# A state-space stage on one core: row statistics moved ahead, the first chunk reordered, sixteen gathers spread over four chunks

## What is computed

```python
x = x + _L0_ffn_ref(_layernorm(x), ...)      # two experts' rows per token are gathered and added
x = x + _L1_attn_ref(_layernorm(x), ...)     # the state space; it adds its own input, the normed x
# _L1_attn_ref(x):
xn = x * rsqrt(mean(x * x) + EPS) * norm_w
xi, res = split(xn @ in_proj_w)
xi = silu(conv1d(xi) + conv_b)               # 4 taps
delta, Bm, Cm = split(xi @ x_proj_w)
delta = softplus(delta @ dt_proj_w + dt_proj_b)
state = exp(delta * -exp(A_log)) * state + delta * Bm * xi    # a scan over 256 steps, 16 states
y = (sum over the states of state * Cm) + xi * D
out = (y * silu(res)) @ out_proj_w + x
```

## Time and profile before

| | us |
|---|---|
| median of 3 runs | 1331.45 |
| lowest, highest | 1325.25, 1331.91 |
| the profiled execution, its own time | 1329.53 |
| its span in the trace | 1327.7 |
| DVE busy in the span | 938.6 (71%) |
| PE busy | 1060.4 (80%) |
| POOL busy | 836.1 (63%) |
| ACT busy | 748.2 (56%) |

### The profile page before, as it was taken

One profiled execution on the slowest core, in us unless ns is written; L12 is line 12 of the kernel. 1 busy time (PEld: TensorE's weight loads), 2 busy tenths in 40 slices (PEclk: granted clock), 3 DMA queues, 4 the chain that ended last, 5 costly groups with the idle time before them and its releaser, 6 DMA issues. The chain is left out here.

```text
span 1327.7 us, 20305 instructions
## 1 busy us (share of the span) xinstructions
PE 1060.4 (80%) x4202; PEld 616.8 (46%) x4203; DVE 938.6 (71%) x2289; ACT 748.2 (56%) x1827; POOL 836.1 (63%) x602
## 2 busy tenths in 40 slices
PE   5888966489999865888988889897774239999995
PEld 4666744367777622323333333333222225555563
DVE  6999998533333325899999999999997525555573
ACT  4768755265555447867677675866422115555542
POOL 2333268657157278968788888879670677347276
PEclk9998878599999977899999999898897559999997
DMA  9994012336335224343445444354440136435345
GB/s 266 156 152 128 1 15 23 36 55 91 64 74 87 61 41 105 128 138 120 159 127 160 126 144 152 119 172 125 150 142 0 41 58 97 78 77 95 77 69 104
DMA packets 140459, 133.22 MB, mean 100 GB/s; under 512 B 14578, under 2 KB 121698, under 8 KB 140258
## 3 DMA queue, kind: packets, MB, share of 16 engines
q1 hardware_dynamic: 107106, 115.55, 33.0%
q0 software_dynamic: 33280, 16.86, 11.4%
HBM read 98.66 MB, written 31.60 MB: 98 GB/s over the span
## 5 line engine op out<-in xcount | busy, mean ns | idle before, releaser
L1766 POOL TENSOR_TENSOR ss_HC<-ss_Hs,ss_Cb 128x512 f32<-128x512 f32 x256 | 317.9, 1272 | 89.9 <-PE ss_Y L1540 68.5
L1540 PE MATMUL ss_Y<-ss_HC,g_ident 128*128 128x512 f32 x512 | 268.0, 641 | 45.7 <-POOL ss_HC L1766 37.9
L1835 DVE TENSOR_TENSOR_SCAN ss_Hs<-ss_dA,ss_dBu 128x512 f32<-128x512 f32 x256 | 297.0, 1201 | 5.4 <-ACT ss_dA L1682 4.9
L852 POOL DMA_INDIRECT rows<-m_XS,g_slot x128 | 181.8, 1420 | 67.1 <-issue 36.2
L1151 PE MATMUL m_x_UP<-g_m_w,m_x_gT 128*128 (+1 forms) x532 | 204.8, 491 | 6.7 <-issue 3.2
L1682 ACT ACTIVATE ss_dA<-ss_delta,g_A 128x510 f32<-128x510 f32 x256 | 167.7, 712 | 57.8 <-DVE ss_Hs L1835 57.6
L1540 PEld LDWEIGHTS ss_Y<-ss_HC,g_ident 128*128 128x128 f32 x512 | 89.5, 196 | 208.8 <-POOL ss_HC L1766 151.4
L1827 DVE TENSOR_TENSOR ss_dBu<-ss_duP,ss_Bb 128x512 f32<-128x512 f32 x256 | 163.1, 683 | 19.2 <-DMA ss_Bb<-bc_rows 14.9
L1171 PEld LDWEIGHTS m_x_DP<-g_m_w,m_x_hT 128*128 128x128 f32 (+1 forms) x908 | 131.5, 189 | 81.2 <-issue 40.1
L1171 PE MATMUL m_x_DP<-g_m_w,m_x_hT 128*128 (+3 forms) x908 | 161.8, 296 | 5.4 <-issue 2.5
L1131 POOL DMA_INDIRECT g_X<-out_rows,g_slot x64 | 99.6, 1557 | 79.9 <-DMA out_rows<-m_x_YO 57.4
(11 more groups left out here) (265 smaller groups left out, 1825.7 us busy)
## 6 DMA issues: line engine op xcount, KB each, us to landing
ss_Bb<-bc_rows SPq DMA_DIRECT2D x64, 512.0 KB, 4.9
ss_Cb<-bc_rows SPq DMA_DIRECT2D x64, 512.0 KB, 3.8
rows<-g_Z SPq DMA_DIRECT2D x2, 5031.0 KB, 55.4
m_x_G<-rows SPq DMA_DIRECT2D x156, 64.5 KB
out_rows<-m_x_YO SPq DMA_DIRECT2D x156, 64.0 KB
g_m_w<-in_w_up SPq DMA_DIRECT2D x1, 2816.0 KB, 10.8
g_m_b<-in_b SPq DMA_DIRECT2D x1, 2160.0 KB, 11.8
g_X<-in_x SPq DMA_DIRECT2D x4, 512.0 KB, 6.5
```

Source lines behind the costliest of these rows:

```text
L852: self.nc.gpsimd.indirect_dma_start(self.XG, bass.IndirectOffsetOnAxis(self.rt.slot[k][:, t:t + 1], 0), self.XS[:, t, :], None, compute_op ...
L1540: ins = nc.tensor.matmul(Yp[:, h, :], ident[:], HC[n % 2][:, h, :], start=False, stop=n == N - 1)
L1766: nc.gpsimd.tensor_tensor(HC[n % 2][:, h, :], Hs[n % 4][:, h, :], Cb[g % 2][:, n % 2, :], ALU.mult).then_inc(hc_ready.sem, 1)
L1835: v_.tensor_tensor_scan(Hs[n % 4][:, h, :], dA[n % NA][:, h, :, :].rearrange("p s t -> p (s t)"), dBu[:, h, :], 0.0, ALU.mult, ALU.add).th ...
```

## The change

Three things are changed.

- A class `StateRows` takes over the row scales, in three batches: tiles 0 to 15, 16 to 23 and 24 to 31. Batch 0 is done in the last steps of the experts: four groups of four `bn_stats` after the steps NX-1 to NX+2, the moments after NX+3, an ACT Sqrt after NX+4, and the reciprocal with its Newton step after NX+5. Batch 1 goes into chunk 0 (DVE after n = 6 and n = 10, ACT after n = 8), batch 2 into chunk 4 (DVE after n = 1 and n = 3, ACT after n = 2). The empty block that waited for the weights is gone; the engines wait themselves.
- The first chunk is reordered. Its gate product moves behind its softplus, chunk 1's rows are normalised early and written to a second xT, the exponential of A moves behind the first silu, and the softplus runs by halves of 512 columns: ACT does Abs, Exp, Identity for one half and then the other, DVE takes the relu, the sums and du by halves. `copy_du` sits between the two halves of dA.
- Of POOL's 32 gathers at the start, 16 stay (tiles 16 to 23). The 16 for tiles 24 to 31 are issued one each after n = 8, 10, 12 and 14 of chunks 0 to 3. `chunks` becomes a plain loop, with no hardware loop.

```diff
+                def closing(s):
+                    if s == NX + 4:
+                        ahead.scalar_root(act, 0)
...
+                def closing(s):
+                    lo, hi = ahead.batches[0]
+                    q = (hi - lo) // 4
+                    if s == NX - 1:
+                        dve.wait_ge(early, 16 * n_early * 2)
+                    if NX - 1 <= s < NX + 3:
+                        ahead.vector_stats(dve, 0, lo + q * (s - NX + 1), lo + q * (s - NX + 2))
+                    if s == NX + 3:
+                        ahead.vector_moments(dve, 0)
+                    if s == NX + 5:
+                        ahead.vector_scales(dve, 0)
...
+    def vector_moments(self, dve, b):
+        v, link = self.nc.vector, Chain(dve, self.chain)
+        lo, hi = self.batches[b]
+        k = hi - lo
+        dve.wait_ge(self.measured.sem, self.measured.after(b))
+        for t in range(k):
+            ins = v.bn_aggr(self.mv[:, t, :], self.st[:, t, :])
+        link(ins)
+        v.tensor_scalar(self.ve[:, 1, 0:k], self.mv[:, 0:k, 1], 1.0 + EPS, EPS * EPS, ALU.mult, ALU.add)
+        v.tensor_scalar(self.ve[:, 0, 0:k], self.mv[:, 0:k, 1], EPS, None, ALU.add).then_inc(self.shifted.sem, 1)
+        v.tensor_copy(self.mean[:, lo:hi], self.mv[:, 0:k, 0])
+
+    def scalar_root(self, act, b):
+        lo, hi = self.batches[b]
+        act.wait_ge(self.shifted.sem, self.shifted.after(b))
+        self.nc.scalar.activation(self.t2[:, :, 0:hi - lo], self.ve[:, :, 0:hi - lo], ACT.Sqrt).then_inc(self.rooted.sem, 1)
+
+    def vector_scales(self, dve, b):
+        v, link = self.nc.vector, Chain(dve, self.chain)
+        lo, hi = self.batches[b]
+        k = hi - lo
+        y, t2 = self.scales[:, :, lo:hi], self.t2[:, :, 0:k]
+        dve.wait_ge(self.rooted.sem, self.rooted.after(b))
+        link(v.reciprocal(y, t2))
+        link(v.tensor_tensor(t2, y, y, ALU.mult))
+        link(v.tensor_tensor(t2, t2, self.ve[:, :, 0:k], ALU.mult))
+        link(v.tensor_scalar(t2, t2, -0.5, 1.5, ALU.mult, ALU.add))
+        link(v.tensor_tensor(y, y, t2, ALU.mult))
+        v.scalar_tensor_tensor(self.shift[:, :, lo:hi], self.mean[:, lo:hi].unsqueeze(1).to_broadcast([P, 2, k]),
+                               -1.0, y, ALU.mult, ALU.mult)
+        v.tensor_scalar(self.lift[:, lo:hi], self.scales[:, 0, lo:hi], 1.0, None, ALU.add).then_inc(self.scaled.sem, 1)
...
+                pe.wait_ge(loaded.sem, loaded.after(n_loaded - 1))
                 turn(0, Q[1])
-                project(0, q)
-                project_gate(0, [dBu[:, h, :] for h in range(2)])
+                project(0, 0, q)
                 pe.wait_ge(weights_ready, 1)
                 pe.wait_ge(padded, 1)
                 for h in range(2):
                     convolve(0, h, q[h])
-                project_dbl(0, 0)
-                project_dt(0)
+                first_dbl(Q[0][0:DT, :], w_lr, (0, 1))
+                first_dbl(Q[1][0:2 * N, :], w_bc, (0,))
+                pe.wait_ge(lr_copied.sem, lr_copied.after(0))
+                nc.tensor.matmul(Q[0][:], w_dt[:, 0:P], lr[:], start=True, stop=True).then_inc(dt_ready.sem, 1)
+                first_dbl(Q[1][0:2 * N, :], w_bc, (1,))
                 turn(1, Z[0])
-                project(1, Z)
+                pe.wait_ge(bc_copied.sem, bc_copied.after(0))
+                nc.tensor.matmul(Q[1][:], w_dt[:, P:2 * P], lr[:], start=True, stop=True).then_inc(dt_ready.sem, 1)
+                pe.wait_ge(xT_copied.sem, xT_copied.after(1))
+                project_gate(0, 0, Z)
+                pe.wait_ge(z_copied.sem, z_copied.after(0))
+                project(1, 1, q)
                 for h in range(2):
-                    convolve(1, h, Z[h])
+                    convolve(1, h, q[h])
...
+                def first_log():
+                    for h in range(2):
+                        act.wait_ge(dt_ready.sem, dt_ready.after(0, h + 1))
+                        nc.scalar.activation(ez[:, h, :], Q[h][:], ACT.Abs, bias=dt_b[:, h:h + 1]).then_inc(first_logs, 1)
+                        act.wait_ge(first_logs, 3 * h + 1)
+                        nc.scalar.activation(ez[:, h, :], ez[:, h, :], ACT.Exp, scale=-1.0).then_inc(first_logs, 1)
+                        act.wait_ge(first_logs, 3 * h + 2)
+                        nc.scalar.activation(tz[:, h, :], ez[:, h, :], ACT.Identity, bias=unit[:, 0:1]).then_inc(first_logs, 1)
+                    for h in range(2):
+                        nc.scalar.activation(ln[:, h, :], ez[:, h, :], ACT.Ln, bias=1.0).then_inc(first_logs, 1)
...
+                        if n == 0 and h == 0 and not at(c, 0, 1):
+                            copy_du(c)
...
+                        if n == 0 and not at(c, 0, 1):
+                            silu_xi(1, 1, q)
+                            silu_gate(0, 0)
...
+                        if (c, n) == (0, 8):
+                            rows_of.scalar_root(act, 1)
+                        if (c, n) == (4, 2):
+                            rows_of.scalar_root(act, 2)
...
+                act.wait_ge(loaded.sem, loaded.after(n_loaded - 1))
                 normalise(0, 0)
-                copy_xT(0, Q[1][:])
+                copy_xT(0, 0, Q[1][:])
+                normalise(1, 0)
                 act.wait_ge(padded, 1)
                 copy_in(0, q)
-                copy_gate(0, 0, [dBu[:, h, :] for h in range(2)])
+                add_normalised(0)
+                add_normalised(1)
                 silu_xi(0, 0, q)
+                nc.scalar.activation(A[:], A[:], ACT.Exp).then_inc(powered, 1)
                 copy_dbl(0)
-                add_normalised(0)
-                copy_dt(0, 0)
                 act.wait_ge(units_set, 2)
-                log_dt(0)
-                normalise(1, 0)
-                add_normalised(1)
-                copy_xT(1, Z[0])
+                first_log()
                 act.wait_ge(negated, 1)
                 act.wait_ge(cleared, NA)
                 powers(0, 0, 0)
-                copy_du(0)
-                for n in range(1, NA - 1):
-                    powers(n, 0, 0)
-                copy_in(1, Z)
-                silu_xi(1, 1, Z)
-                silu_gate(0, 0)
+                copy_in(1, q)
+                powers(1, 0, 0)
+                copy_gate(0, 0, Z)
+                powers(2, 0, 0)
                 chunks(act, scan)
...
-                for k in range(2):
-                    for t in range(n_early, T):
-                        nc.gpsimd.indirect_dma_start(X[:, t * D:(t + 1) * D], None, Y,
-                                                     bass.IndirectOffsetOnAxis(rt.slot[k][:, t:t + 1], 0),
-                                                     compute_op=ALU.add).then_inc(gathered, 16)
-                    pool.wait_ge(gathered, 16 * (T - n_early) * (k + 1))
+                def gather(k, t, done):
+                    nc.gpsimd.indirect_dma_start(X[:, t * D:(t + 1) * D], None, Y,
+                                                 bass.IndirectOffsetOnAxis(rt.slot[k][:, t:t + 1], 0),
+                                                 compute_op=ALU.add).then_inc(done, 16)
+
+                for t in range(*soon):
+                    gather(0, t, gathered)
+                pool.wait_ge(gathered, 16 * n_soon)
+                for t in range(*soon):
+                    gather(1, t, gathered)
 
...
+                        i = 4 * c + (n - 8) // 2
+                        if n >= 8 and n % 2 == 0 and i < 2 * n_late:
+                            if i == n_late:
+                                pool.wait_ge(late_gathered, 16 * n_late)
+                            gather(i // n_late, late[0] + i % n_late, late_gathered)
...
+                        if (c, n) == (0, 6):
+                            dve.wait_ge(gathered, 16 * 2 * n_soon)
+                            rows_of.vector_stats(dve, 1, *soon)
+                            rows_of.vector_moments(dve, 1)
+                        if (c, n) == (0, 10):
+                            rows_of.vector_scales(dve, 1)
+                        if (c, n) == (4, 1):
+                            dve.wait_ge(late_gathered, 16 * 2 * n_late)
+                            rows_of.vector_stats(dve, 2, *late)
+                            rows_of.vector_moments(dve, 2)
+                        if (c, n) == (4, 3):
+                            rows_of.vector_scales(dve, 2)
...
+                def first_relu(h):
+                    dve.wait_ge(first_logs, 3 * h + 1)
+                    v_.tensor_scalar(delta[0][:, h, :], Q[h][:], dt_b[:, h:h + 1], 0.0, ALU.add, ALU.max).then_inc(z_copied.sem, 2)
+
+                def first_rest(h):
+                    dve.wait_ge(first_logs, 3 * h + 3)
+                    v_.scalar_tensor_tensor(tz[:, h, :], tz[:, h, :], -1.0, ez[:, h, :], ALU.add, ALU.subtract).then_inc(first_sums, 1)
+
+                first_relu(0)
+                dve.wait_ge(turned.sem, turned.after(1))
```

(15 more changed lines are left out.)

150 lines of the change are left out of this document (57 added, 93 removed).

## The result

The changed kernel took 1316.38 us (median of 10 runs, 1313.25 to 1320.61), the kernel before 1331.37 us beside it: ratio 0.9894, 95% interval 0.9874 to 0.9913, so between 11.6 and 16.8 us less (15.0 by the medians). 1317.2 was forecast. The profiled execution took 1313.25 us (span 1311.3), against 1329.53 (1327.7).

The account below looks back on a forecast made before the run. DVE was taken to set the pace. Gains of 7.6, 1.6, 8.2 and 3.3 less losses of 6.0 and 2.4 made 12.3 us, from 1329.53 to 1317.2 us; forecast 1312 to 1323, 8 in 10 range 1307.5 to 1328.

Parts of the forecast that it names:

- Row scales of half 0: Stage start: batch 0's scales move into the experts' last steps and are hidden there; gain 7.6 us.
- Gate product: Head: without the gate product on PE ahead of it, the convolution starts 2.65 us earlier; gain 1.6 us.
- the reserve of 1.0 us for a slower start: Head: part of PE's convolution runs at the lower clock; 1.0 us taken off the gate product's gain.
- Softplus by halves: Head: second silu's end to DVE's first product takes 14.1 us instead of 22.3; gain 8.2 us.
- POOL's start: Stage start: 16 fewer gathers free 29.4 us on POOL, giving back only what its lateness cost in chunk 0.
- Chunk 0: First chunk: 8.0 us of waits, now for ACT, instead of 8.8, and cheaper row scales; gain 3.3 us.
- Chunk 4: Chunk 4: the last batch's small DVE operations, held up by POOL, are new there; loss 6.0 us.
- Gathers in chunks 1 to 3: Four gathers per chunk on POOL delay products and loads by 0.8 us per chunk; loss 2.4 us.
- The sum: Whole kernel: all gains and losses together gain 12.3 us, from the profiled 1329.53 to 1317.2 us.
- POOL did not become the bound: Rival, chunks 0 to 3: gathers add in full, 25.9 us instead of 2.4, giving 1340.7 us; chance 0.08.
- Rival 2: Chunks: both batches cost 10.6 us, each chunk with gathers 3; no change, 1331 us; chance 0.17 for the whole corner.
- rival 3: Chunks: gathers free, small operations at idle price, chunk 0's waits halved; gain 23 us, 1306.5; chance 0.15.

Follow-up runs that it names:

- e1: Changed kernel with batch 0's row scales back at the start of the state-space stage: 1323.56 us.
- e3: Changed kernel with the first chunk's old order on TensorE, ScalarE and VectorE; row scales stay ahead, gathers spread: 1330.45 us.
- e2: Changed kernel with all 32 gathers issued at the start of the stage: 1328.06 us.
- e9: Changed kernel with batch 1's row sums, means and variances behind chunk 0's fourth scan, not the seventh: 1315.32 us.
- e10: Changed kernel with batch 2's root ahead of the dt copies and its scales behind chunk 4's third scan, not the fourth: 1315.71 us.
- e4: Changed kernel without the 16 gathers spread over chunks 0 to 3, so part of the computation is missing: 1314.40 us.
- e5: Changed kernel with the 16 late gathers moved to where POOL waits: ten in chunk 0, two each in chunks 1 to 3: 1320.86 us.
- a2: The changed kernel timed and profiled once more, no edit: 1315.09 us.
- e8: Changed kernel with chunk 0's powers of states 4 to 6 earlier on ACT and the first gate's silu behind state 12: 1312.39 us.
- e11: Changed kernel with the edits of e9, e10 and e5 together: 1310.51 us.
- e6: Changed kernel with batch 2's scales in chunk 4 one state later, behind the fifth scan: 1314.83 us.
- e14: e11 with batch 1's scales behind chunk 0's fourteenth scan, not the eleventh: 1314.43 us.

## Why the prediction was right

- **Row scales of half 0, 7.6.** e1 gives 8.15. The two normalisation starts (0.07 and 7.76 us behind the memset) show the same.
- **Gate product, 1.6.** The convolution stands 2.58 us earlier behind the normalisation and takes 0.93 longer: 1.65. The granted clock was 0.54 in the convolution's first 2.04 us and 1.00 behind them, where it had been 1.00 from its start before: the reserve of 1.0 us for a slower start was of the right size.
- **Softplus by halves, 8.2.** 7.5: 14.8 us in place of 14.1. Together with the gate product e3 gives 9.85 for 9.8. That the old order costs 5.6 us more in chunk 0 as well the prediction did not have: 1.4 of waits for ACT, and mostly one short operation held up.
- **POOL's start, nothing by itself.** Right only with the rest unchanged: in the changed kernel the 16 gathers at the start would cost 10.7 us (e2), since the shorter head is what uncovers them. The three parts undone singly cost 8.0, 10.7 and 16.5 us, 35 in sum, while all together gained 10.75. Even without the 4.7 us of e3's one operation the sum is over 30: the parts are conditions for each other, and the sum of a step list is not a sum of single effects.
- **Chunk 0, 3.3.** It fell by 3.3 us. Waits for ACT 7.98 (8.0 forecast), at n = 4 and 6 instead of n = 6 alone; the prediction's own list already has the power of n = 4 ready at 18.4, 3.4 us behind its scan's nominal 15.0. Row scales: 6.44 from 523.60 to 530.04, and 1.25 for the scales at n = 10, together 7.7, the number forecast. This match is luck in part: the scales met an idle POOL, and the same seven operations at the same n took 5.9 us in e3 and 7.0 in e9.
- **Chunk 4, a loss of 6.0.** The term that was mis-sized. The sums took 3.5 us (counted with chunk 3 by my marks) and chunk 4 rose by 4.0. In it stand the seven operations (3.3 us) and a wait of 3.98 that I did not have: the root stands on ACT behind the log of the next chunk. Against them its waits for B and PE, 2.8 us before, are gone.

```profile
765.66 0.25 DVE L1406 RECIPROCAL g_scales<-sr_t 128x16 f32<-128x16 f32 x1 [3.98 <-ACT sr_t L1398]
```

  So 7.5, and 1.5 came back in chunks 5 to 7: the net 6.0 equals the forecast by two misses that cancel. e10 removes the wait and the contention.
- **Gathers in chunks 1 to 3, a loss of 2.4.** e4 gives 2.3 (1.7 for the stage). The way was another: not B, whose waits in chunks 1 to 3 fell from 6.1 to 5.5 us, but the gate product. POOL's last products, late by the gathers, make PE's last sum late:

```profile
631.97 1.23 DVE L1873 TENSOR_TENSOR ss_yg<-ss_Y,ss_gate 128x1024 f32<-128x1024 f32 x1 [2.41 <-PE ss_Y L1604]
```

  It waited 0.60 before, in e4 0.73 and in e5 0.83. Chunks 1 to 3 rose by 6.9 us in all. With 3.5 for the sums and 2.3 for the gathers 1.1 is left, and no term of the prediction has it: chunk 1 takes 60.15 us in e4, without any late gather, against 58.82 before. So chunks 1 and 3, with 61.9 and 62.1 us, lie outside the 59 to 61 forecast for each.
- **The sum, 12.3.** The stage gained 10.75 and, by the second profile, 11.4: the head 16.9 (17.4 forecast), chunk 0 3.3 (3.3), and the chunks behind it lost 9.4 (8.4). One barrier less gives 0.4. The spans of the two profiles differ by 16.4; the rest, 3.5 us ahead of the stage and 1.7 behind it, is in parts that the change leaves alone, and a2 shows that the first moves by as much from one execution to the next. The forecast of 1317.2 us stands 0.8 from the median, so closer than its terms deserve: it was taken off an execution 1.9 under the median of the kernel before, and by the medians the gain is 15.0 us, 2.7 more than forecast, while the stage gave 0.9 to 1.6 less. Whether 3 us or so of the measured gain belong to something outside the stage stays open. There is only one profile of the kernel before, and the experiments point both ways: e2, with a stage as long as in that profile, takes as long as the kernel before (ratio 0.9996), but e3, with a stage 5.7 us longer, does nearly so too (1.0010).

Of the rivals, POOL did not become the bound (25.9 us of loss were priced for the gathers, 2.3 came), yet e8, e9 and e11 show it one step behind: take away ACT's waits or move DVE's work and POOL or its port takes most of the gain. Rival 2 priced a batch at 10.6 us with POOL busy throughout; e6, e9 and e14 show that price nearly (7.4, 7.0 and 6.5 us for the scales alone). In rival 3 one term is a slip: half of chunk 0's 8.0 us of waits is 4, not 3, which would put it at 1305.5 us.

## What to carry to other kernels

Undo each part of a change alone before crediting it: parts that shorten one chain and relieve another engine may each be worthless without the other. Short VectorE operations between SBUF tiles cost what GpSimd is doing at that moment, so place them where the trace shows GpSimd idle, and look again after every other move, since the place shifts. A wait that the profile puts down to one engine can be the cover of another: before paying for its removal, see when the next engine's work for the same point is done.

## What the hardware showed that I had not expected

- A short VectorE operation on SBUF (128x8 or 128x16, 0.16 to 0.19 us alone) is held up not always for one GpSimd instruction, as by the rule quoted under e6, but at times through an unbroken row of them: 9.98 us in e5, 5.37 in e11, 4.83 in e3, 3.78 in e9. In e6 and e14 each was let in after one. All four rows began right behind a gather on GpSimd or with it, without idle time between, and from there its records overlap (in e5 softplus steps 2.90 us long, the next product 2.32 behind their start); rows that began after an idle time, as at 551.99 in e14, let the operation in after one or two instructions. What of this decides was not tried.
- `bn_stats`, `bn_aggr` and the reciprocal ran at the same length beside GpSimd as without (1.62, 0.64 and 0.22 to 0.25 us).
- A stretch of this program repeats to a few hundredths between kernels (61.87, 61.85, 61.85 and 61.89 for chunk 1 in four of them) and then jumps by 1.3 us in one execution (60.55), with the next chunk taking it back.
